# A scan over 16 states: the next tile's preparation begins two steps earlier, and two of the 16 input products move to GpSimd

## The reference, cut to what matters

```python
xc = silu(conv(xh)); dt, Bm, Cm = split(xc @ x_proj_w.T)
delta = softplus(dt @ dt_proj_w.T + dt_proj_b)
h = h * exp(delta[:, None] * A) + (delta * xc)[:, None] * b[None, :]   # 128 channels, 16 states
y = (h @ c + xc * D) * silu(z)
out = silu(layernorm(y @ out_proj_w.T @ proj_w.T + proj_b)) + x
```

## Time and profile before

| what | value |
| --- | --- |
| median of 3 runs (lowest, highest) | 13125.51 us (13124.51, 13127.3) |
| the profiled execution's own time | 13120.83 us |
| its span, first to last instruction | 13119.0 us |
| instructions | 161233 |
| VectorE, TensorE, ScalarE, GpSimd busy in the last 4119 us | 3924.54, 3608.33, 3142.45, 3238.33 us |

### The profile page before, as it was taken

The page is one execution under the profiler, slowest core; times in us unless marked ns, Lnnn a source line. Parts: engine busy times, 40 slices in busy tenths (PEclk is TensorE's granted clock), DMA queues, the critical chain, the costliest instruction groups (busy, mean ns, idle before and its releaser), DMA issues.

```text
span 13119.0 us, 161233 instructions
## 1 busy us (share of the span) xinstructions
PE 11668.5 (89%) x34287; PEld 4280.2 (33%) x34287; DVE 10235.9 (78%) x13211; ACT 7905.5 (60%) x12824; POOL 7307.1 (56%) x5412
## 2 busy tenths in 40 slices
PE   4989899999989998888888888888888888888888
PEld 1333333333333333333333333333333333333333
DVE  6454545455454439999999999999999999999999
ACT  1333333333333337777777777777777777777777
POOL 6030303022030007777777777777777777777777
PEclk9989899999989999999999999999999999999999
DMA  2010100101010003333333433333343343333333
GB/s 56 2 27 2 27 9 21 28 2 27 2 27 2 1 10 150 151 144 147 155 144 144 156 146 144 151 151 144 147 155 144 144 155 147 144 152 150 144 149 153
DMA packets 372433, 1297.68 MB, mean 99 GB/s; under 512 B 177904, under 2 KB 177904, under 8 KB 231792
## 3 DMA queue, kind: packets, MB, share of 16 engines
q1 hardware_dynamic: 372336, 1296.81, 26.8%
HBM read 1246.07 MB, written 50.56 MB: 99 GB/s over the span
## 4 chain that ended last, share of the span: by engine, by line
PE 22%; issue 15%; ACT 14%; DVE 9%; POOL 1%; ACTq 0%; DVEq 0%; POOLq 0%; DMA 0%; SPq 0%
PE ybank L1133 7%; ACT da L1033 6%; DVE bbank L904 5%; DVE h L918 3%; PE bbank L1123 2%; PE ubank L1087 2%; PE pbank L1109 2%; PE vbank L1084 2%; PE vbank L1085 2%; PE vbank L1091 2%; PE ubank L1093 2%; PE ybank L1131 2%; ACT av L977 1%; ACT e L989 1%; ACT ev L984 1%
## 5 line engine op out<-in xcount | busy, mean ns | idle before, releaser
L838 POOL TENSOR_TENSOR pr<-h,cc 128x512 f32<-128x512 f32 x4110 | 5201.5, 1269 | 1381.4 <-DVE h L918 1380.1
L918 DVE TENSOR_TENSOR_SCAN h<-da,h,bbank 128x512 f32<-128x512 f32 x4110 | 5198.8, 1265 | 0.0
L1133 PE MATMUL ybank<-pr,m_small 128*128 128x512 f32 x8214 | 4195.6, 597 | 0.0
L904 DVE TENSOR_TENSOR bbank<-bbank,du 128x512 f32<-128x512 f32 x4111 | 2766.5, 673 | 44.6 <-PE bbank L1123 10.0
L432 ACT ACTIVATE prob<-st 128x512 f32<-128x512 f32 x2048 | 1222.7, 597 | 2575.1 <-PE st L564 2575.1
L1033 ACT ACTIVATE da<-dl,a 128x512 f32<-128x512 f32 x4114 | 2736.4, 712 | 17.1 <-DVE dl L886 1.1
L307 DVE TENSOR_REDUCE mpart<-s 128x1 f32<-128x512 f32 x2048 | 1322.2, 686 | 1089.5 <-PE s L530 1081.0
L1123 PE MATMUL bbank<-bcs,selb 96*128 96x512 bf16 x4113 | 1556.5, 389 | 646.7 <-DVE h L918 623.9
L564 PE MATMUL st<-qf,kf 65*128 (+1 forms) x4096 | 2121.3, 620 | 5.9 <-ACT qf L436 5.9
L240 POOL TENSOR_TENSOR rowsum<-xin 128x1024 f32<-128x1024 f32 x64 | 153.5, 2398 | 2994.4 <-PE vb L597 2905.0
L1133 PEld LDWEIGHTS ybank<-pr,m_small 128*128 128x128 f32 x8214 | 1561.0, 194 | 678.7 <-issue 597.6
(11 more groups left out here) (153 smaller groups left out, 11693.5 us busy)
## 6 DMA issues: line engine op xcount, KB each, us to landing
cc<-c_rows SPq DMA_DIRECT2D x1032, 1024.0 KB, 7.9
upw<-up SPq DMA_DIRECT2D x260, 256.0 KB, 9.5
xin<-x SPq DMA_DIRECT2D x128, 512.0 KB, 6.8
out<-ot SPq DMA_DIRECT2D x256, 128.0 KB, 2.3
zw<-zn_tokens SPq DMA_DIRECT2D x780, 32.0 KB, 9.8
c_rows<-crows SPq DMA_DIRECT2D x258, 32.0 KB, 1.6
zn_tokens<-znb SPq DMA_DIRECT2D x64, 128.0 KB, 2.0
a_small<-small SPq DMA_DIRECT2D x1, 1331.0 KB, 5.6
```

The costliest lines, as they stand in the source:

```text
L838: pool.tensor_tensor(pr[:, n % 8, :], h[:, n, :], cc[par][:, n, :], ALU.mult).then_inc(prod_done, 1)
L904: dve.tensor_tensor(bbank[n % 4][:, :], bbank[n % 4][:, :], du[par][:, :], ALU.mult)\
L918: dve.tensor_tensor_scan(h[:, n, :], da[:, n % 8, :], bbank[n % 4][:, :], h[:, n, TB - 1:TB], ALU.mult, ALU.add).then_inc(scan_done, 1)
L1133: pe.matmul(ybank[:, :], w("ident"), pr[:, n % 8, :], start=False, stop=(n == S - 1))\
```

## The change

States 4 and 12 (POOL_B) get their B rows like the rows of C: `crow` in DRAM has two more rows, a fifth broadcasting DMA of 512 KB a tile loads them into `cc[par][:, 16:18]`, and GpSimd multiplies them by `du` into `dbp`, three steps before their scan. VectorE's `inputs` and TensorE's `spread_b` skip these states. Their decay goes to `bbank[0]` in PSUM, which is free then, and ScalarE makes it at step n itself, no longer four states ahead.

All of `prep` is moved up. The `u` matmuls and copies of tile t + 1 stand behind steps 14 and 15 of tile t - 1 (n = -2, -1), the convolution behind step 0 (before: 2), `xc` behind step 1 (before: 3), the softplus chain behind step 4 (before: 6), `cv` and `l2` behind 6 and 7 (before: 8 and 9), `dl` behind 10 (before: 11), `du` behind 11 (before: 12). The gate `sz` is made one tile later than before, in the same place in the order, from the running tile's `u2`. Several tiles of the softplus chain share memory (`ev` is `av`, `lv` and `l2` are `e1`, `cv` is `ed`), with waits for that, and the table of small operands is loaded in part only. The first layer is the same.

```diff
+POOL_B = (4, 12)
+NB = len(POOL_B)
+OWN = [n for n in range(S) if n not in POOL_B]
...
-        ct = crows[96:96 + S, :]
+        ct = crows[96:96 + S + NB, :]
         av = sb("av", [P, TB])
-        ev = sb("ev", [P, TB])
+        ev = av
         e1 = sb("e1", [P, TB])
         ed = sb("ed", [P, TB])
-        lv = sb("lv", [P, TB])
-        cv = sb("cv", [P, TB])
-        l2 = sb("l2", [P, TB])
+        lv = e1
+        cv = ed
+        l2 = e1
...
-        cc = [sb(f"cc{i}", [P, S, TB]) for i in range(2)]
+        cc = [sb(f"cc{i}", [P, S + NB, TB]) for i in range(2)]
+        dbp = sb("dbp", [P, NB, TB])
...
+                if not first:
+                    sp.wait_ge(dbp_done, (tau - 1) * NB)
+                sp.dma_start(cc[par][:, S:S + NB, :].rearrange("p n t -> p (n t)"),
+                             crow[par:par + 1, S * TB:(S + NB) * TB].broadcast_to([P, NB * TB]))\
+                  .then_inc(b_in[par], 16)
...
-                if n == 8:
+                if n == 6:
...
-                if n == 9:
+                if n == 7:
...
-                if n == 12:
+                if n == 11:
...
-                if n == 6:
+                if n == 4:
                     residual(g, 1 - s, k)
...
+            def inputs(k, g, par, count, first):
+                pool.wait_ge(b_in[par], count * 16)
+                if not first:
+                    pool.wait_ge(scan_done, (g - 1) * S + POOL_B[k] + 1)
+                pool.tensor_tensor(dbp[:, k, :], cc[par][:, S + k, :], du[par][:, :], ALU.mult).then_inc(dbp_done, 1)
...
                 c = g * S + n
+                if n + 3 in POOL_B:
+                    inputs(POOL_B.index(n + 3), g, par, count, first)
...
-                if n == 11:
+                if n == 10:
...
+                    dve.wait_ge(sz_done, g + 1)
                     dve.tensor_tensor(yb[:, :], ybank[:, :], sz[s][:, :], ALU.mult).then_inc(yb_done, 1)
...
-                dve.wait_ge(bb_mm, g * S + n + 1)
+                if n in POOL_B:
+                    return
+                dve.wait_ge(bb_mm, g * len(OWN) + OWN.index(n) + 1)
...
-                dve.wait_ge(db_done, c + 1)
-                dve.wait_ge(da_done, c + 1)
+                if n in POOL_B:
+                    dve.wait_ge(dbp_done, g * NB + POOL_B.index(n) + 1)
+                else:
+                    dve.wait_ge(db_done, g * len(OWN) + OWN.index(n) + 1)
+                dve.wait_ge(da_done, g * S + DECAYS.index(n) + 1)
                 if not first:
                     dve.wait_ge(prod_done, c - S + 1)
-                dve.tensor_tensor_scan(h[:, n, :], da[:, n % 8, :], bbank[n % 4][:, :], h[:, n, TB - 1:TB],
+                if n in POOL_B:
+                    decay, inp = bbank[n % 4][:, :], dbp[:, POOL_B.index(n), :]
+                else:
+                    decay, inp = da[:, n % 8, :], bbank[n % 4][:, :]
+                dve.tensor_tensor_scan(h[:, n, :], decay, inp, h[:, n, TB - 1:TB],
                                        ALU.mult, ALU.add).then_inc(scan_done, 1)
...
-                if n == 1:
+                if n == -1:
...
-                if n == 3:
+                if n == 1:
                     act.wait_ge(conv_mm, tau + 1)
                     if not first:
                         act.wait_ge(sum_mm, (tau - 1) * S)
                         act.wait_ge(du_done, tau - 1)
                     act.activation(xc[par][:, :], vbank[:, :], ACT.Silu, bias=w("convb")).then_inc(xc_done, 1)
-                    act.wait_ge(z_mm, tau + 1)
-                    if not first:
-                        act.wait_ge(yb_done, tau - 1)
-                    act.activation(sz[par][:, :], ubank[:, :], ACT.Silu).then_inc(sz_done, 1)
+                    if not start:
+                        act.wait_ge(z_mm, tau)
+                        if not first:
+                            act.wait_ge(yb_done, tau - 2)
+                        act.activation(sz[1 - par][:, :], ubank[:, :], ACT.Silu).then_inc(sz_done, 1)
                     if not first:
                         finish(tau - 2)
                     act.preload_act_table_set(LN_EXP)
-                if n == 6:
+                if n == 4:
                     act.wait_ge(v_mm, tau + 1)
+                    act.wait_ge(cv_done, tau)
                     act.activation(av[:, :], vbank[:, :], ACT.Abs, bias=w("dtb")).then_inc(abs_done, 1)
...
-                        act.wait_ge(bb_mm, (tau - 1) * S)
+                        act.wait_ge(bb_mm, (tau - 1) * len(OWN))
                     act.copy(bcs[par][:, :], ubank[0:96, :]).then_inc(hi_done, 1)
                     act.wait_ge(abs_done, tau + 1)
-                    act.wait_ge(cv_done, tau)
                     act.activation(ev[:, :], av[:, :], ACT.Exp, scale=-1.0).then_inc(ev_done, 1)
...
-                    act.copy(ct, ubank[96:96 + S, :]).then_inc(ct_done, 1)
+                    act.copy(ct, ubank[96:96 + S + NB, :]).then_inc(ct_done, 1)
                     act.wait_ge(ev_done, tau + 1)
+                    act.wait_ge(dl_done, tau)
                     act.activation(e1[:, :], ev[:, :], ACT.Identity, bias=1.0).then_inc(e1_done, 1)
                     act.wait_ge(l2_done, tau)
                     act.wait_ge(e1_done, tau + 1)
+                    act.activation(ed[:, :], e1[:, :], ACT.Identity, bias=-1.0).then_inc(ed_done, 1)
+                    act.wait_ge(ed_done, tau + 1)
                     act.activation(lv[:, :], e1[:, :], ACT.Ln).then_inc(lv_done, 1)
-                    act.activation(ed[:, :], e1[:, :], ACT.Identity, bias=-1.0).then_inc(ed_done, 1)
-                if n == 7:
+                if n == 5:
                     act.activation(vbank[:, :], vbank[:, :], ACT.Relu, bias=w("dtb")).then_inc(rv_done, 1)
-                if n == 8:
+                if n == 6:
                     act.wait_ge(rest_mm, tau + 1)
                     act.copy(bcs[par][0:64, :], ubank[0:64, :]).then_inc(mid_done, 1)
-                if n == 10:
+                if n == 8:
                     act.wait_ge(last_mm, tau + 1)
                     act.copy(bcs[par][0:32, :], ubank[0:32, :]).then_inc(bcs_done, 1)
...
-                if n == 0:
+                if n == -2:
...
-                if not first or n >= 8:
-                    act.wait_ge(scan_done, c - 7)
-                act.activation(da[:, n % 8, :], dl[par][:, :], ACT.Exp, scale=a[:, n:n + 1]).then_inc(da_done, 1)
+                if n in POOL_B:
+                    if not first or n >= 4:
+                        act.wait_ge(scan_done, c - 3)
+                    to = bbank[n % 4][:, :]
+                else:
+                    if not first or n >= 8:
+                        act.wait_ge(scan_done, c - 7)
+                    to = da[:, n % 8, :]
+                act.activation(to, dl[par][:, :], ACT.Exp, scale=a[:, n:n + 1]).then_inc(da_done, 1)
             def step(n, g, par, first):
+                if n in POOL_B:
+                    decay(n, g, par, first)
                 if n + LEAD < S:
-                    decay(n + LEAD, g, par, first)
+                    if n + LEAD not in POOL_B:
+                        decay(n + LEAD, g, par, first)
...
+                            post(n - S, g, s)
+                            prep(n - S, g + 2, s, b * PAIRS + i + s + 1, False, False)
...
-                if n == 2:
+                if n == 0:
                     pe.wait_ge(u2_done, tau * 2 + 2)
                     pe.wait_ge(dl_done, tau)
                     pe.matmul(vbank[:, :], tapw[:, 0, :], u2[par][:, 2:2 + TB], start=True, stop=False)
                     pe.matmul(vbank[:, :], tapw[:, 1, :], u2[par][:, 0:TB], start=False, stop=True)\
                       .then_inc(conv_mm, 1)
-                    pe.matmul(ubank[:, :], w("inT")[0:64, P:2 * P], u2[par][0:64, 2:2 + TB], start=True,
-                              stop=True).then_inc(z_mm, 1)
-                if n == 5:
+                    if not start:
+                        pe.matmul(ubank[:, :], w("inT")[0:64, P:2 * P], u2[1 - par][0:64, 2:2 + TB], start=True,
+                                  stop=True).then_inc(z_mm, 1)
+                if n == 3:
                     pe.wait_ge(xc_done, tau + 1)
                     pe.matmul(vbank[:, :], wdl[:, :], xc[par][:, :], start=True, stop=True).then_inc(v_mm, 1)
-                    pe.wait_ge(sz_done, tau + 1)
+                    pe.wait_ge(sz_done, tau)
                     pe.matmul(ubank[:, :], w("xpT"), xc[par][:, :], start=True, stop=True).then_inc(bc_mm, 1)
-                if n == 7:
...
+                if n in POOL_B:
+                    return
...
+                            prep(n - S, g + 2, s, b * PAIRS + i + 2)
```

More of the change, by code:

```diff
@@ L623 @@
 LAG = 3
+POOL_B = (4, 12)
+NB = len(POOL_B)
+OWN = [n for n in range(S) if n not in POOL_B]
+DECAYS = sorted(range(S), key=lambda n: n if n in POOL_B else n - LEAD + 0.5)
 def mamba_phase(nc, zn, crow, small, sel, up, out):
@@ L640, in sem, with w @@
```

(45 more changed lines are left out.)

3 lines of the change are left out of this document (2 added, 1 removed).

## The result

The changed kernel took 13755.17 us (median of 4 runs, 13750.86 to 13757.63) against 13125.01 before: a ratio of 1.048, 95% interval 1.0461 to 1.0498. It is slower by 630 us, 2.46 us for each of the 256 tiles.

What follows compares the result with a forecast made beforehand. VectorE was taken as the bound, busy 3924.54 of the last 4119 us. Per tile a new wait of 5.07 less savings of 2.75, times 256, adds 594 us to 13120.83: 13715, range 13370 to 13970.

Steps and rivals of the forecast that it cites:

- The savings: VectorE, per tile: two input products 1.17, the wait at `dl` 1.37, the small B row wait 0.21; together 2.75 us.
- The new wait: VectorE's scan 4 waits for ScalarE's late decay of state 4: 5.07 us a tile.
- The table load stands behind the wait: ScalarE: the table load for `xc` starts only after the preceding tile's 16 sums, putting its 1.30 us on the chain.
- Rival A: ScalarE's table load runs ahead of the wait: a wait of 3.77 us, 13382 in all; chance 0.11.
- Rival D: ScalarE runs empty ahead of both table loads: wait 2.6 us longer, 14380 (14420 by the skill page); chance 0.01.
- The rest of the tile: From scan 4 to the end of scan 15: 21.39 us, the decay of state 12 in time; tile 34.07 us.
- some tenths: ScalarE's decay of state 12 is ready at A + 13.9, VectorE's scan 12 due at A + 14.2 (A: scan 4's start).
- rival B: TensorE matmuls at half clock after idling, or state 12's decay a microsecond late: 256 us more, 13970; chance 0.14.
- the same clock: TensorE's busy share falls from 88% to near 80% while its granted clock stays the same.
- if the scan over a PSUM decay is slower than 1.26: VectorE: a sign that the forecast is wrong, since it took the scan's 1.26 us as unchanged.
- Rival C: ScalarE is held only by older, finished sums, so state 4's decay is in time: 12417; chance 0.08.

Runs made afterwards that it cites:

- run 7: Changed kernel, but xc waits only for the preceding tile's skip-term matmul and both PSUM decays are issued three steps ahead of their scans: 12399.18 us.
- run 1: Changed kernel, but the decay of state 4 is issued at ScalarE's step 1, ahead of the table load for xc: 13795.69 us.
- run 2: Changed kernel, but both PSUM decays (states 4 and 12) are issued three steps ahead of their scans: 13743.89 us.
- run 5: Changed kernel without the B move: all B rows on TensorE, all input products on VectorE, decays four ahead; preparation stays earlier: 13708.83 us.
- run 3: Changed kernel, but xc waits only for the preceding tile's skip-term matmul, not for all 16 sums: 12903.91 us.
- run 9: Kernel before the change, but xc waits only for the preceding tile's skip-term matmul, not for its 16 sums: 13122.29 us.
- run 4: Changed kernel with all preparation back at its old steps; states 4 and 12 stay on GpSimd, their PSUM decays at step n: 14061.26 us.
- run 6: Changed kernel with preparation at its old steps, states 4 and 12 on GpSimd, their decays issued three steps ahead: 13356.69 us.
- run 10: Changed kernel, but TensorE's convolution and gate matmul stand behind the last sum (step 2), as before the change: 13709.34 us.

## Why the prediction was right

The forecast was 13715, the measurement 13755.

- **The savings** (1.17 + 1.37 + 0.21 = 2.75 a tile). Right, shown by run 7: a tile of 28.98 where 28.97 was worked out. `dl` waits for nothing in the changed kernel.
- **The new wait** (5.07). Measured 5.20. The last sum ends at E + 6.22 instead of 6.13; the sum of state 14, the first one behind the gate, takes 0.97 until the next instruction and not 0.86. From the table load to scan 4 it is 6.51, worked out as 6.50. This is 0.13 of the 0.14 us a tile by which the forecast fell short (2.32 against 2.46). That nothing else seems to be missing is luck: two more differences of 0.12 cancel. The mean tile before is 31.84 and not 31.72, for which the prediction's own have the count. And 26 of the changed kernel's tiles take 34.9 to 35.8 instead of 34.2, some 30 us in all.
- **The table load stands behind the wait.** Shown: it starts 0.07 us after the last sum ends, and `xc` follows at once. Rival A falls. Rival D falls too: from the end of `so` (9026.58) to the first decay (9027.89) it is 1.31 us, which leaves 0.03 for anything but the load. By the rule of the Trainium skill (page "ScalarE: Activation LUTs", section "What ACT_TABLE_LOAD costs") a drain of 1.38 should come with each; the trace, with its 0.03, does not agree with that part.
- **The rest of the tile.** The decay of state 12 ends at 9009.46, scan 12 starts at 9009.89: in time by 0.4 us, as "some tenths" said. The margin is too small in the 26 long tiles: in one of them TensorE waits 1.68 us for `bcs` (8967.83), its variance matmul takes 1.97 us (8970.18), and the input product of state 13 and scan 12 wait 0.97 and 0.38 (8974.62, 8975.70). This is rival B, with 30 us and not 256.
- **Clock and shares.** Here I was off: not "the same clock", 80% busy, but 0.95 and 85% (4058.06 of 4753). The wait for `xc` on TensorE (1.89 us) is followed by pairs of nearly twice the length. Behind this wait they fall in the time that VectorE waits anyway and cost nothing; rival B named the effect, but for the stretch ahead of the last sum, where the rows are at the full rate.
- **A sign set too sharp.** The forecast was to be wrong "if the scan over a PSUM decay is slower than 1.26". It takes 1.278 on average against 1.265, which is 0.03 us a tile at most; in run 7, where no scan waits, it is 1.267 against 1.262. The sum doesn't change.
- **The cause, put more exactly.** The prediction named the late decay of state 4. Runs 1, 2 and 5 show that this is where the loss appears first: issue it early, or do away with it, and 13700 to 13800 stay, at the B rows. What stands behind it is one count in one semaphore wait, met two steps earlier than before (runs 3 and 9: 851 us with the changed order, 0 with the old one). The late decays are a second cause, hidden by the first. Made early they bring 11 us while the wait for 16 sums stands (run 2) and 505 once it is gone (run 3 against 7); in the old order, where that wait costs nothing, the B move costs 937 us with late decays and 233 with early ones (runs 4 and 6). Rival C's mechanism, ScalarE not held by the sums of the preceding tile, is real; the kernel as changed doesn't have it. Run 3 gives it, but its decays are still late by 1.67; with early decays it comes to 12399, where C said 12417.

Open: how much of the B row waits in runs 1, 2, 5 and 6 is TensorE's order (a B row behind a correction that waits for ScalarE) and how much the lower clock that follows such a wait. They come together in these four. Run 10 tells them apart for one wait: with the same order and the same 1.68 us, the tiles in which matmuls of nearly double length follow are 1.3 us longer. Why they follow in one tile and not in the next stays open.

## What to carry to other kernels

When work is moved earlier in a queue, look at each wait in front of it: one that cost nothing in its old place is met that much sooner, and everything behind it in the queue inherits the difference. Ask then what the wait protects; here a buffer was free 16 sums before the count said so, and the exact count turned a loss of 630 us into a gain of 221. And making the first waiter disappear may gain nothing (11 us in run 2), or much, once another wait is gone (505 us): work out who is next behind the same late engine, on all engines that take their instructions in order, before promising the gain.

## What the runs showed of the hardware

- A scan that reads its decay from PSUM and its input from SBUF took 1267 ns in run 7, one with the roles exchanged 1262 ns. In the changed kernel it is 1278 against 1265, but there half of the first kind stand behind a wait.
- GpSimd did 22 operations a tile beside a VectorE that was busy without a gap (run 7: 3743.32 and 4000.00 of 4000 us), and both kept the durations of the kernel before (product 1271 against 1269 ns, scan 1262 against 1265).
- On TensorE, matmul pairs of 1.02 to 1.12 us took up to 2.07 us for some microseconds behind some waits, and not behind others of the same length. From 8000 to 12000 us, one or more of the next eight matmuls had nearly double length behind 104 of 116 waits of 1.89 us in the changed kernel, behind 36 of 117 waits of 1.68 us in run 10, and behind 8 of 126 waits of 1.38 us in the kernel before. In run 4 the pair behind a wait of 2.14 us (9011.26) kept its 1.02. The granted clock in this stretch was 0.95 in the changed kernel, 0.91 in run 1, 0.97 in run 10, and 1.00 in run 7, where the longest wait of TensorE is 1.3 us.
